# Two attention blocks in a row: values of a half's first step alone in the first and last round, usual gaps for block 1, sooner projections of the second image

## The reference

```python
# block 0, x: (16, 128, 1024)
h = group_norm(x, 32 groups) * scale + bias
q, k, v = h Wq + bq, h Wk + bk, h Wv + bv        # 4 heads of 32 channels
w = softmax(q.k / sqrt(128))                     # 1024 x 1024 for each head
x = (x + (w v) Wp + bp) / sqrt(2)
# block 1
h = group_norm(x, 8 groups) * w + b
q, k, v = split(h qkv_w.T + qkv_b)               # one head of 128 channels
x = x + softmax(q.k / sqrt(128)) v proj_w.T + proj_b
```

## Time and profile before

| | |
|---|---|
| median of 3 runs | 1640.89 us (1640.61 to 1641.0) |
| profiled execution, its own time | 1639.49 us |
| its span | 1637.7 us, mean granted TensorE clock 0.987 |
| busy | PE 1576.2 (96%), POOL 1189.6 (73%), DVE 1144.1 (70%), ACT 1095.7 (67%) |
| round 0 | about 43.8 to 124.3 us of the span |
| round 15 | about 1469.4 to 1562.8 us of the span |

### The profile page before, as it was taken

One profiled execution on the slowest core, in us unless ns is written; L12 is line 12 of the kernel. 1 busy time (PEld: TensorE's weight loads), 2 busy tenths in 40 slices (PEclk: granted clock), 3 DMA queues, 4 the chain that ended last, 5 costly groups with the idle time before them and its releaser, 6 DMA issues.

```text
span 1637.7 us, 26098 instructions
## 1 busy us (share of the span) xinstructions
PE 1576.2 (96%) x9511; PEld 1094.9 (67%) x9511; DVE 1144.1 (70%) x1961; ACT 1095.7 (67%) x1858; POOL 1189.6 (73%) x563
## 2 busy tenths in 40 slices
PE   7888999999999999999999999999999999999998
PEld 5434667667667766766676766767667676765567
DVE  7567776777777777777777777677777767765242
ACT  1445777676677776767777677777767776765655
POOL 2687977788587787868789687778868777887610
PEclk7889999999999999999999999999999999999999
DMA  6504041140413205041231414114141410400000
GB/s 180 153 20 122 20 120 50 40 110 20 129 40 90 59 33 136 21 129 40 75 75 33 118 38 129 40 54 96 33 117 40 118 51 26 111 20 7 7 7 20
DMA packets 47662, 111.72 MB, mean 68 GB/s; under 512 B 5808, under 2 KB 6448, under 8 KB 47536
## 3 DMA queue, kind: packets, MB, share of 16 engines
q1 hardware_dynamic: 47248, 109.86, 24.3%
q10 hardware_dynamic: 288, 0.20, 0.0%
HBM read 67.84 MB, written 41.94 MB: 67 GB/s over the span
## 4 chain that ended last, share of the span: by engine, by line
PE 83%; DVE 6%; DMA 5%; ACT 3%; issue 2%; SPq 0%; POOL 0%; ACTq 0%; POOLq 0%
PE bank L1073 13%; PE scores L1041 13%; PE acc L998 13%; PE scores L980 12%; PE scores L1028 6%; PE scores L1020 4%; DVE halfmax L859 4%; PE scores L1021 3%; PE bank L1090 3%; PE scores L1022 3%; DMA k_stack<-parts_dram 3%; PE bank L1108 2%; PE bank L1112 2%; DMA parts_dram<-k_lo 1%; PE acc L1080 1%
## 5 line engine op out<-in xcount | busy, mean ns | idle before, releaser
L627 POOL TENSOR_TENSOR sum<-sum,probs 128x1024 f32<-128x1024 f32 x444 | 1043.2, 2381 | 280.8 <-PE acc L998 268.6
L859 DVE TENSOR_REDUCE halfmax<-bank 128x1 f32<-128x512 f32 x968 | 631.8, 680 | 208.5 <-PE bank L1073 208.2
L675 ACT ACTIVATE probs<-scores 128x512 f32<-128x512 f32 x896 | 515.6, 600 | 204.4 <-PE scores L980 198.6
L980 PE MATMUL scores<-q_stack,k_stack 97*128 97x512 f32 x1024 | 436.2, 437 | 3.2 <-issue 1.4
L1073 PE MATMUL bank<-k_stack,q_stack 96*128 96x512 f32 x952 | 384.0, 425 | 13.7 <-DVE halfmax L859 6.3
L1073 PEld LDWEIGHTS bank<-k_stack,q_stack 96*128 96x128 f32 x952 | 176.2, 190 | 148.5 <-DVE halfmax L859 65.2
L1041 PEld LDWEIGHTS scores<-v,turned 128*128 128x128 f32 x1952 | 251.1, 192 | 30.5 <-ACT turned L695 14.0
L1041 PE MATMUL scores<-v,turned 128*128 128x128 f32 x1952 | 258.2, 277 | 4.4 <-ACT turned L695 3.8
L980 PEld LDWEIGHTS scores<-q_stack,k_stack 97*128 97x128 f32 x1024 | 194.1, 191 | 58.3 <-issue 27.4
L998 PE MATMUL acc<-probs,v 128*32 128x512 f32 x1792 | 220.4, 603 | 0.0
L898 DVE TENSOR_REDUCE negmax<-scores 128x1 f32<-128x1024 f32 x128 | 156.7, 1224 | 68.8 <-PE scores L1022 66.5
(11 more groups left out here) (121 smaller groups left out, 1600.9 us busy)
## 6 DMA issues: line engine op xcount, KB each, us to landing
q_stack<-parts_dram SPq DMA_DIRECT2D x96, 256.0 KB, 5.2
k_stack<-parts_dram SPq DMA_DIRECT2D x96, 256.0 KB, 7.6
xin<-x_dram SPq DMA_DIRECT2D x16, 512.0 KB, 3.5
x<-x_dram SPq DMA_DIRECT2D x16, 512.0 KB, 3.5
parts_dram<-q_hi SPq DMA_DIRECT2D x16, 512.0 KB, 2.6
parts_dram<-q_lo SPq DMA_DIRECT2D x16, 512.0 KB, 3.5
parts_dram<-k_hi SPq DMA_DIRECT2D x16, 512.0 KB, 2.6
parts_dram<-k_lo SPq DMA_DIRECT2D x16, 512.0 KB, 3.6
```

The source lines that it names most:

```text
L627: pool.tensor_tensor(total, total, probs[:, ring_slot(i, half, kt), 2 * two:2 * two + 2, :], ALU.add).then_inc(added[two], 1)
L675: act.activation(dst, score_bank(i, index), ACT.Exp).then_inc(exp_done, 1)
L859: dve.tensor_reduce(halfmax[:, h, t, half:half + 1], banks[p][:, :], AX.X, ALU.max).then_inc(bank_free[p][VE], 1)
L980: pe.matmul(score_bank(i, index), ks[0:SPLIT + 1, i % 2, h, tile(kt)], qs[0:SPLIT + 1, q_half(i, half), h, :], start=True, stop=True).then ...
```

## The change

Three edits to the tables; no instruction is added or taken away.

- Round 0 and round 15 take the values of step 0 and of step 8 alone: `pv 4` at gap 43 becomes `pv_a 4` at gap 39 and `pv_b 4` at gap 43. `pv 0` was already two pieces; in round 15 its `pv_a` moves from gap 5 to gap 8.
- Round 0 does the second image's projections sooner: on PE `q0` halves at gap 5 and 5 (before 7 and 8), `k0` at 6 and 7 (before 8 and 10), `v0` at 11 and 20 (before 14 and 21). ACT's parts follow at the same gaps, DVE's low parts at 5, 5, 8 and 8 (before 7, 8, 8 and 10).
- Round 15 takes block 1's pieces of the middle rounds in place of `end_tile_pieces`: `turn` on PE and ACT one gap sooner, `pv1a` two gaps and `pv1b` one gap sooner on PE, `oevict` one gap sooner on ACT, `exp1` of even tiles one gap later on ACT. Tile 2 of image 14 so ends in round 15 and not at gap 0 of round 16. `exp1` of tile 7 comes ahead of `save`, and `turn` of tile 5 ahead of `proj`. `out` of gap 16 moves to 13, `affine1` from 30 to 27, `norm1` from 33 to 31.

The deal of the PSUM banks shifts with the order (for example `v0` of the second image waits for one use less of its bank).

```diff
-ROUND_FIRST = [p for p in ROUND if (p[0] not in ("max", "gather", "shift") or p[2]) and p[:3] != ("pv", 0, 0)] + [
-    ("pv_a", 0, 0, 5, None, None), ("pv_b", 0, 0, 11, None, None), ("v0", 1, 0, 1, 1, None)] + [
+EARLY_VALUES = [("pv_a", 0, 0, 5, None, None), ("pv_b", 0, 0, 11, None, None),
+                ("pv_a", 4, 0, 39, None, None), ("pv_b", 4, 0, 43, None, None)]
+EARLY_PAIRS = [("pv", n, 0) for n in (0, 4)]
+FIRST_PROJECTIONS = [
+    ("q0", 0, 1, 5, 5, 5), ("q0", 1, 1, 5, 5, 5), ("k0", 0, 1, 6, 6, 8), ("k0", 1, 1, 7, 7, 8),
+    ("v0", 0, 1, 11, 11, None), ("v0", 1, 1, 20, 20, None),
+]
+ROUND_FIRST = [p for p in ROUND if (p[0] not in ("max", "gather", "shift") or p[2]) and p[:3] not in EARLY_PAIRS
+               and p[:3] not in [q[:3] for q in FIRST_PROJECTIONS]] + EARLY_VALUES + FIRST_PROJECTIONS + [
+    ("v0", 1, 0, 1, 1, None)] + [
...
-def end_tile_pieces(t, offset, first):
-    return [("score1", (t, 0), offset, first, None, None), ("score1", (t, 1), offset, first + 1, None, None),
-            ("max1", t, offset, None, None, first + 1), ("exp1", t, offset, None, first + 1, None),
-            ("rinv", t, offset, None, None, first + 3), ("turn", t, offset, first + 4, first + 4, None),
-            ("pv1a", t, offset, first + 7, first + 7, None), ("pv1b", t, offset, first + 7, None, None)]
...
-END_PIECES = [("out", 0, -2, 16, None, 16), ("pv_a", 0, 0, 5, None, None), ("pv_b", 0, 0, 11, None, None),
-              ("affine1", 0, -1, None, None, 30), ("norm1", 0, -1, None, 33, None)]
-ROUND_END = [p for p in ROUND if p[0] not in TILE_PIECES and p[:3] != ("pv", 0, 0)
-             and p[:3] not in [q[:3] for q in END_PIECES]] + END_PIECES
+END_PIECES = [("pv_a", 0, 0, 8, None, None)] + EARLY_VALUES[1:] + [
+    ("affine1", 0, -1, None, None, 27), ("norm1", 0, -1, None, 31, None)]
+ROUND_END = [p for p in ROUND if p[:3] not in EARLY_PAIRS and p[:3] not in [q[:3] for q in END_PIECES]] + END_PIECES
...
-LATER = [p for p in END_TILES if p[2] == -2 and tile_of(p) < LAST_TILE]
-ROUND_END += [p for p in END_TILES if p not in LATER]
+LATER = [p for p in folded(BLOCK1) if p[2] == -2 and p[0] != "out" and tile_of(p) < LAST_TILE]
```

More of the change, by code:

```diff
@@ L175 @@
-END_AT = {(n % KT, n // KT - 2): TILE_FIRST + TILE_GAPS * n - GAPS for n in range(3, 3 + KT)}
-TILE_PIECES = ("score1", "max1", "exp1", "rinv", "turn", "pv1a", "pv1b")
-END_PIECES = [("out", 0, -2, 16, None, 16), ("pv_a", 0, 0, 5, None, None), ("pv_b", 0, 0, 11, None, None),
-              ("affine1", 0, -1, None, None, 30), ("norm1", 0, -1, None, 33, None)]
-ROUND_END = [p for p in ROUND if p[0] not in TILE_PIECES and p[:3] != ("pv", 0, 0)
-             and p[:3] not in [q[:3] for q in END_PIECES]] + END_PIECES
@@ L182 @@
-END_TILES = folded([p for (t, offset), first in END_AT.items() for p in end_tile_pieces(t, offset, first)])
+END_PIECES = [("pv_a", 0, 0, 8, None, None)] + EARLY_VALUES[1:] + [
+    ("affine1", 0, -1, None, None, 27), ("norm1", 0, -1, None, 31, None)]
+ROUND_END = [p for p in ROUND if p[:3] not in EARLY_PAIRS and p[:3] not in [q[:3] for q in END_PIECES]] + END_PIECES
 DIRECT = 2
```

## The result

The change makes the kernel faster: 1628.2 us median of 4 runs (1626.31 to 1630.01) against 1640.75 us of the kernel before (4 runs, 1639.36 to 1641.0), ratio 0.9925 with a 95% interval of 0.9908 to 0.9942. That is 12.5 us where I had forecast 6.5, outside my range (1630.5 to 1640.0). Over all comparisons, this one and the later ones, the kernel before has a mean of 1639.0 us (80 runs, between 1633 and 1645) and the change 1628.7 us (10 runs), so some 10.3 us is the steadier figure, and about 2 us of the first were scatter. The direction was right and so was the split into two rounds; the size for round 15 was not, nor, as the experiments show, all of the reasons for it.

A forecast was written before the change was run, and what follows sets the result against it. PE, busy 96% of the span, was taken as the bound, so only its idle and slow times could be won. Round 0's 2.95 us plus round 15's 3.6 gave 6.5, so 1634.4 us, range 1630.5 to 1640.0.

The forecast's parts named there:

- (E): Round 0, values of step 8 alone at gap 39: POOL's chain starts sooner; gain 1.8 us, between 1.3 and 2.3.
- (D): Round 0, second image's projections sooner: last `k_lo` 1.5 us sooner; gain taken as 1.3 us, between 0.8 and 1.8.
- (a): Round 15, gaps 3 to 10: turn goes ahead and step 0's values come after ACT's save; gain 1.2 us.
- (b): Round 15, gaps 11 to 18: the stretch is DVE's and order changes nothing of its sum; gain 0.3 us.
- (c): Round 15, mean of block 1: `pv1a` now stands between it and the projection; gain 0.4 us.
- (d): Round 15, shift's DMA wait: covered by `pv1a` and `pv1b`, but the turn delays the shift; gain 0.3 us.
- (e): Round 15, tile 7 to tile 1: `exp1` of tile 7 no longer behind the save; gain 1.7 us.
- (f): Round 15, tiles 1 and 2: sooner eviction in tile 1, projection covers a wait in tile 2; gain 0.5 us.
- Splitting: Round 15: splitting `pv1` costs about 0.08 us eight times and splitting the values 0.15; term -0.8 us.
- Only round 0 pays: Rival: round 15's waits belong to a tile's serial loop, so order changes little; 1637.7 us; chance 0.25.
- The clock: Rival: round 0's PE idle gets too short for the clock to fall; up to 2.3 us more, 1632.1; chance 0.1.
- Slower: Rival: in round 15 `pv1a` stalls behind its eviction, 6.4 us over eight tiles; 1644.4 us; chance 0.15 with other losses.

The follow-up runs named there:

- e8: The change, with the four reciprocals of image 0's first half behind the shift in round 0 (DVE gaps 58 to 60, not 49 to 56); 1630.84 us, ratio 0.9951.
- e2: The kernel before with only the change's round 15 edits, round 0 as before; 1631.66 us, ratio 0.9961.
- e1: The kernel before with only the change's round 0 edits, round 15 as before; 1638.58 us, ratio 0.9996.
- e4: The kernel before with only the sooner projections of round 0; 1637.36 us, ratio 0.9992.
- e6: The kernel before with only round 0's values of step 8 alone at gap 39 and step 9 at gap 43; 1637.95 us, ratio 0.9994.
- e9: The change, with block 1's turn one gap later on PE and ACT in round 15; round 15 to the end 164.7 us, 160.3 with the change.
- e5: The whole change run once more against the kernel before; 1628.78 us, ratio 0.9943.
- e17: The change, with the values of steps 8 and 9 in one piece at gap 43 in round 15; 1628.94 us, ratio 0.9941.
- e12: The change, with `pv_a 0` of round 15 at gap 5 again; round 15 to the end 161.5 us, 160.3 with the change.
- e14: The kernel before, its gap numbers kept, block 1's pieces ahead inside their gap in round 15; round 15 to the end 165.1 us, 167.8 before.
- e10: The kernel before, with usual gaps for tiles 3 to 5 of image 13 and `out` at 13; round 15 to the end 167.1 us, 167.7 before.
- e15: e10, with those three tiles' pieces also at their place in `ROUND`, ahead inside their gap; round 15 to the end 164.3 us, 167.8 before.
- e13: The change, with block 1's pieces last inside their gap in round 15; round 15 to the end 165.1 us, 160.3 with the change.
- e11: The change, with `pv1a` one gap later on PE, beside `pv1b`, in round 15; 1631.42 us, ratio 0.9958.

## Why the prediction was wrong, step by step

**Round 0, 2.95 us: about right by the profiles, less sure by whole runs.** From the first exponential of round 0 to that of round 2 the eight profiles with the old `ROUND_FIRST` take 168.8 to 173.7 us, mean 170.8, the eight with the full new one (e8 left out) 165.6 to 170.3, mean 167.8: 3.0 us, with a standard error of 0.7. Over whole runs the change is 3.2 us below e2 (1628.7 and 1631.9), while e1 is only 0.5 below before, each with a standard error of about 0.9; the two parts by themselves (e4 and e6) give 1.6 and 1.3. A gain of 2 to 3 us fits best, and no run here settles it closer. Of the parts, (E) does what it should: the wait for the mix is gone, and L0 is 77.6 in e6 against 79.2 as the mean of the old ones. (D) brought the last `k_lo` to 57.24 in the kernel after, 2.5 us sooner, where I had rebuilt 1.5; but counted from the round's first exponential it came 12.6 us behind in four profiles and 14.1 in the other six, against 15.2 before. In those four the values of step 0 took 1.06 us, in the others 1.6 to 1.9: it goes with the granted clock at that point (from 49.5 to 52.0 us it is 1.00 in the kernel after and in e9, 0.79 before, 0.76 in e5, 0.50 in e17). Slow with slow, D brings that `k_lo` 1.1 us sooner, a little under my estimate. The profile after was one of the lucky four, and the profile before had the shortest round 1 but one of all (88.9 us; the others 88.7 to 93.8), so no single pair of profiles shows round 0 rightly.

**Round 15: 7.5 in place of 3.6 us.** The terms by the table of maxima:

- (a) gaps 3 to 10: 2.6 where I had 1.2. I listed 0.85 at the save and 0.6 at maxima as removable, and PE's idle there fell by about that, 1.6 us; I then took off 0.3 for a new wait at `pv1a` that isn't there (the turn's lead over `pv1a` keeps it out), and the other 1.0 us is PE's busy time, which I had left as it was. e12 gives 1.2 of it to `pv_a` at gap 8.
- (b) gaps 11 to 18: 1.5 where I had 0.3. This is the step that failed most clearly, in its mechanism and not only in its size. I called the stretch DVE's, from a wait of 0.91 for `halfmax`, and said that the order changes nothing of DVE's sum. DVE's sum is the same, but PE was waiting for one single maximum while a turn of 0.8 us stood behind it. With the new order alone (e14) or the new gap number alone (e10) the wait stays 0.91; e15, with both, takes it away, and e13 brings it back.
- (c) tile 5 to 6: 0.5 where I had 0.4, and (d), 6 to 7: 0.0 where I had 0.3. In (d) the shift's DMA is covered, and the wait turned up at `pv1a` (0.53), as I had feared.
- (e) tile 7 to 1: 2.4 where I had 1.7. The exponential of tile 7 follows its maximum directly, as forecast, and none of the large waits is left there.
- (f) from tile 1 on: 0.5, as forecast in sum. The serial loop of tile 1 got no shorter (9.38 us, before 9.32, where I had rebuilt 9.2); what was gained lies behind the maximum of tile 2, where the wait of 0.64 has gone.
- Splitting, -0.8: the wrong sign. The values of step 8 cost 0.3 (e17), but `pv1a` apart and a gap sooner gives 1.7 us (e11), since it fills waits. The 0.08 for each `pv1` was misread too: the rows that I named give 2 x 1.06 - 2.02 = 0.10.

Two things lie under these. **The order inside a gap** was not in my list of edits: I read the gap numbers in the table and not the place of the pieces in the list. Without it the change would give 2.7 us in round 15 (e13), which is near what I forecast, for partly wrong reasons.

**PE's busy time isn't fixed by its work.** I had added idle only. From the first exponential to the maximum of tile 2 PE does the same work in these four kernels. Busy time by engine over that stretch (columns as in the earlier trace rows), in order before, e10, e15 and after:

```profile
1469.93:1555.26 85.33, 78.65 (x465) 49.10 (x463) 38.26 (x63) 54.74 (x98) 60.23 (x29) 1.00 0.02 7
1469.44:1554.07 84.63, 77.22 (x465) 49.17 (x463) 38.49 (x63) 54.90 (x98) 60.10 (x29) 1.00 0.02 7
1469.95:1551.86 81.91, 76.46 (x465) 49.67 (x463) 38.22 (x64) 55.12 (x98) 60.11 (x29) 1.00 0.02 8
1467.93:1546.36 78.43, 76.49 (x465) 49.73 (x463) 38.32 (x64) 56.56 (x98) 61.39 (x30) 1.00 0.02 8
```

Part of the 2.2 us is that a wait costs more than its bracket. In the rows a matmul of 512 columns in a run starts 0.23 to 0.24 us behind the one before, while the last ahead of a wait has its full 0.40 and the first behind it takes 0.50. Such an end is modelled by the profile, so this says how much of a wait the profile books as busy time. The Trainium skill (TensorE: Matmul & The Clock Gate, Single matmul latency) states for a single bf16 matmul that it takes (398 + N)/2.4 ns at the full clock, N being its columns, and (Back-to-back issue gap) that one behind another starts N/2.4 + 2.5 ns later; by an estimate from these, a break costs some 0.16 us. The rows are near it (0.40 less 0.23). I did not use it. But a fixed price for each wait does not fit all runs: before and e10 have thirteen waits above 0.2 us in this stretch, with 1.4 us between their busy times, and e15 has ten where after has three, with the same busy time. The order of the pieces changes busy time in other ways too, and what they are stays open.

**The rivals.** Only round 0 pays: excluded by e2. The clock: it stayed low behind the 3.43 us (0.56, 0.52), as the wait did. Slower: excluded as a whole, but its price is real where the turn comes late (e9, 4.4 us). The rule on program order: I had said that by it a turn put sooner can only move the wait unless other work takes its place. That condition is met, and I didn't see it: the turn itself is the other work, since DVE goes on with its maxima while PE transposes (e15).

**The range.** My upper bound for round 15 was 5.5 us, the idle less three evictions. With PE's busy time 2 us lower, as measured, that bound would have been about 7.5, and the range would have reached down to about 1628.5. The rest of the miss in the first comparison, 2 us, is the scatter of whole runs, which three runs within 0.4 us of each other had hidden.

What stays open: why the values of step 0 run at the full clock in four of the ten profiles with the sooner projections and in none of nine without. The work ahead of it is the same in both, so it may be chance.

## What to carry to other kernels

When a table gives an order, read the final list of instructions and not the numbers: which piece stands ahead of which inside one slot was worth as much here as the slots. A wait for one result with ready, unrelated work right behind it is not the other engine's bound; put that work ahead and the other engine catches up. In this kernel the order inside a slot and the slot number worked only together in the first half of the round, so test both. Don't take TensorE's busy time as fixed when you bound a gain by its idle time: it fell here by 2 us with the same matmuls. When whole runs scatter by several us, compare the length of the stretch that was changed: it repeated here to 0.01 us for the new round 15 and to 0.1 us for the old one, in profiles whose clock stayed up there; look at the clock before you compare.

## What was unexpected of the hardware

In one of nineteen profiles the clock dropped in round 15, just behind a short wait; that the wait caused it isn't shown. In e1 a wait of 0.86 us before the values of step 0 in round 15, the same as before, was followed by slower values (1.74 us against 1.06) and a turn at nearly half pace (1.97 against 1.09). PE in order of time, and busy time of that stretch, e1:

```profile
1475.76 1.74 PE L1006 MATMUL acc<-sum,v 128*32 128x512 f32 x8 [0.86 <-issue]
1477.43 1.97 PE L1036 MATMUL scores<-consts,probs 128*128 128x128 f32 x8
```

```profile
1475.40:1479.40 4.00, 3.64 (x17) 2.16 (x18) 0.30 (x1) 0.26 (x1) 1.75 (x1) 0.58 0.00 0
```

L15 there is 169.3 in place of the 167.7 to 167.8 of e4, e6 and before: 1.5 us for a clock of 0.58 over 4 us, so for most of them at the lower level, 1.2 GHz. The same place has a clock of 1.00 in e6, and so it has in e12 behind a longer wait, 1.43 us. Round 1 varies by 5 us between the profiles (88.7 to 93.8), and rounds 2 to 14 together by 4 us (1254.4 to 1258.8); neither shows a link to the change, and so one profile stands for the median only within several us.
